# A fused linear-attention and mixture-of-experts layer: the state faded by two diagonal matrix products on PE, the gate split in two products, one normalisation chain for two uses

## The chip, the cores and the metric

The kernel runs on one core of a Trainium2 chip. The metric is the device time of one execution in microseconds (us). Engines are named as in the profile: PE (TensorE), PEld (its weight loads), DVE (VectorE), ACT (ScalarE), POOL (GpSimd) and SP (SyncE, which issues transfers).

## The reference, cut to what matters

The input x is 2 x 2048 x 256 in float32. A linear attention with a decaying state is followed by a gated mixture of experts (8 experts, two per token).

```python
def attn(out, W_write, W_read, decay, log_alpha):      # 4 heads of 64
    v = out @ W_write.T                                # values, per head
    # wk = out shifted by one token; M[p, q] = gamma**(p - 1 - q) where p > q
    # per chunk of tokens:
    #   reads = (W @ rk) * gamma**p  +  ((rk wk^T) * M) @ v
    #   W     = gamma**C * W  +  (v * gamma**(C-1-p))^T @ wk
    return out + (alpha * reads) @ W_read.T

def ffn(x, gate_w, w1, b1, w2, b2):
    probs = softmax(x @ gate_w.T)
    topk_probs, topk_idx = top_k(probs, 2)
    h = gelu(x @ w1[:, e] + b1[e])                     # for the two experts e
    return sum(topk_probs * (h @ w2[:, e] + b2[e]))

x = x + attn(layernorm(x))
x = x + ffn(layernorm(x))
```

## The kernel before, in words

The 2048 tokens of both batch rows are cut into 16 chunks of 128 tokens (`NCH = 16`); a chunk holds two matrices of 128 x 256. Stage one runs over the chunks as a software pipeline written out by hand. Each engine has a function `step(n)`, and in step n it works on several chunks at once: chunk n is normalised, chunk n-1 turned (transposed on PE), chunk n-2 goes through scores, values, state and reads, chunk n-3 through the read projection and the second layer norm, and chunk n-4 and n-5 through the gate, the choice of experts and the places of the rows in a sorted table in DRAM. Engines run their own queues in order and wait for each other by semaphores: `reached(engine, name, m)` waits until `name` has been signalled for chunk m.

Names that the text uses, with lines of the kernel before:

- `turn_chunk` (PE, L1546) transposes chunk n-1. `chunk_high` (ACT, L725) casts it to fp16, and `chunk_low` (DVE, L1036) computes what the cast left over; `last_column` is L736 and L738 on ACT. All products with three fp16 parts use such halves.
- `project` (PE, L1509) is the read projection, `residual` (DVE, L985) adds it, `residual_stats` (L992) and `residual_moments` (L1000) are the second layer norm's statistics.
- `values` (PE, L1573), `weigh` (PE, L1559) are values and scores; `weigh_scores` (DVE, L1052) multiplies scores with the decay table; `reads` (PE, L1592 and L1599) needs it and the state. `states` (PE, L1612) makes a chunk's contribution, `carry` (DVE, L1027) fades the state and adds it.
- `turn_normed` (PE, L1496), `normed_transposed` (ACT, L639), `score_experts` (PE, L1520) and `logits` (DVE, L1007) are the gate's product. `largest` (DVE, L891 to L897), `choose`, `exponential` (ACT, L654), `rank` (PE, L1533 to L1536), `place` (DVE, L960 to L978) follow.
- `normalise` (ACT, L673) and `chunk_normalise` (ACT, L702) apply the two layer norms; POOL makes their factors in a chain L546, L547, L549 (a power of -1/2), L551, once for each norm and step, and scatters rows to DRAM (L559).
- A weight split is the cast of 1024 columns of expert weights into two fp16 halves: `split_high` (ACT, L632) and `split_low` (DVE, L874). `PIECES` gives their number in each step: three in steps 3 to 7, two in steps 8 to 15, none in step 16.

PE's `step` issues, in this order, for the chunks named: turn_chunk(n-1), project(n-3), turn_normed(n-4), values(n-2), weigh(n-2), rank(n-5), states(n-2), score_experts(n-4), reads(n-2).

Stage two multiplies tiles of 256 or 128 sorted rows with the experts' weights (L1697 first layer, L1712 and L1714 second), in groups (`pair(f, z)`: group f of the first layer, group z of the second). Its first tiles use a table made after step 16 from the chunks placed by then. The last chunks' gate work stands between the first groups.

## Time and profile before

| what | value |
|---|---|
| median of three runs | 563.22 us (561.47 to 564.38) |
| profiled execution | 562.67 us |
| its span, first to last instruction | 560.9 us |
| PE busy | 530.1 us (95%) |
| DVE busy | 448.4 us (80%) |
| ACT busy | 338.3 us (60%) |
| POOL busy | 246.9 us (44%) |

The profiled execution's own time is 1.8 us over its span, the work around the program. Busy shares are means over two stages: up to about 167 us the chunks are worked on, and from there to the end PE multiplies with the experts' weights without a gap to speak of.

### The profile page before, as it was taken

The page shows a single profiled execution, that of the slowest core. Times are in us where ns is not written, and L with a number is a line of the kernel's source. Part 1 is how long each engine was busy: PE and PEld are TensorE (multiplying, and loading weights), DVE is VectorE, ACT ScalarE, POOL GpSimd, SP SyncE. Part 2 cuts the span into 40 slices and gives each one's busy share as a digit, 9 for nine tenths or more (in the row PEclk, how much of TensorE's full clock was granted, in tenths as well). Part 3 has the DMA queues.
Part 4 walks back from the last instruction along what each step waited for, and adds up shares of the span by engine and source line. Part 5 has one row for each costly group of instructions (what it writes and reads, how often), then busy time and mean ns, then how long its engine had stood idle before and what let it go on. Part 6 is the DMA issues. An engine that isn't in the chain of part 4 may idle for free.

```text
span 560.9 us, 17645 instructions
## 1 busy us (share of the span) xinstructions
PE 530.1 (95%) x5234; PEld 415.3 (74%) x5234; DVE 448.4 (80%) x1375; ACT 338.3 (60%) x856; POOL 246.9 (44%) x291
## 2 busy tenths in 40 slices
PE   7799899999999999999999999999999999999991
PEld 7677778778786777777777777777777777777770
DVE  4889999999987689868768787688777777778861
ACT  6899989898745876445545554455544544545540
POOL 5625778888746084523223233223322333322433
PEclk9999999999998999999999999999999999999997
DMA  5576867777345396433263364343344454344323
GB/s 161 201 229 225 258 185 234 210 222 231 126 105 129 87 216 101 71 60 62 51 103 56 53 105 77 63 68 61 61 63 79 78 78 75 68 64 67 63 37 36
DMA packets 85096, 63.33 MB, mean 113 GB/s; under 512 B 54224, under 2 KB 77392, under 8 KB 85008
## 3 DMA queue, kind: packets, MB, share of 16 engines
q1 hardware_dynamic: 71328, 43.94, 32.3%
q0 software_dynamic: 13392, 18.27, 17.3%
q8 instruction: 49, 0.80, 0.6%
q14 instruction: 39, 0.32, 0.2%
q10 hardware_dynamic: 288, 0.00, 0.0%
HBM read 37.56 MB, written 24.62 MB: 111 GB/s over the span
## 4 chain that ended last, share of the span: by engine, by line
PE 77%; DVE 10%; issue 4%; DMA 3%; ACT 2%; POOL 1%; SPq 1%; POOLq 0%; DVEq 0%; ACTq 0%
PE psum L1697 32%; PE psum L1712 21%; PE psum L1714 10%; PE psum L1509 3%; DVE weights L874 2%; PE psum L1592 2%; PE psum L1573 2%; PE psum L1599 2%; PE psum L1520 2%; DVE arena L1052 1%; PE psum L1559 1%; DMA arena<-sent_rows 1%; PE psum L1612 1%; PE psum L1496 1%; DVE arena L1063 1%
## 5 line engine op out<-in xcount | busy, mean ns | idle before, releaser
L1697 PE MATMUL psum<-arena,weights 128*128 128x256 f16 (+1 forms) x2208 | 279.7, 249 | 1.1 <-DVE arena L1316 1.0
L1697 PEld LDWEIGHTS psum<-arena,weights 128*128 x2208 | 187.4, 98 | 79.3 <-issue 4.1
L589 POOL DMA_INDIRECT out<-arena,tile_in x71 | 115.0, 1619 | 233.4 <-DVE arena L1343 126.9
L1712 PE MATMUL psum<-weights,arena 128*128 x556 | 211.7, 381 | 0.0
L826 ACT ACTIVATE arena<-psum,b_cur 128x256 f32<-128x256 f32 (+1 forms) x368 | 131.4, 423 | 129.9 <-PE psum L1697 115.6
L1714 PE MATMUL psum<-weights,arena 128*128 x556 | 152.0, 273 | 0.0
L1327 DVE TENSOR_TENSOR arena<-arena 128x512 f16<-128x512 f32 x142 | 98.5, 694 | 10.8 <-ACT arena L843 6.3
L559 POOL DMA_INDIRECT sent_rows<-arena,tiny x64 | 65.4, 1022 | 35.5 <-issue 17.8
L1323 DVE CAST arena<-arena 128x512 f16<-128x512 f32 x126 | 53.5, 424 | 8.8 <-ACT arena L826 8.5
L1712 PEld LDWEIGHTS psum<-weights,arena 128*128 128x128 f16 x556 | 54.4, 98 | 5.0
L1714 PEld LDWEIGHTS psum<-weights,arena 128*128 128x128 f16 x556 | 54.5, 98 | 4.6
L1309 DVE STREAM_TRANSPOSE tileT<-arena 128x512 f32<-128x512 f32 (+1 forms) x46 | 27.0, 586 | 37.1 <-DMA arena<-sent_rows 37.0
L647 ACT ACTIVATE arena<-tileT 128x512 f16<-128x512 f32 (+1 forms) x46 | 24.4, 531 | 49.8 <-DVE tileT L1309 49.8
L1339 DVE SCALAR_TENSOR_TENSOR arena<-psum,gate_scaled,arena 128x256 f32<-128x256 f32 x71 | 34.1, 480 | 15.5 <-PE psum L1714 13.8
L874 DVE SCALAR_TENSOR_TENSOR weights<-weights 128x1024 f16<-128x1024 f32 x32 | 38.5, 1215 | 2.0 <-ACT weights L632 2.0
L1509 PE MATMUL psum<-wrT,arena 128*128 128x256 f32 x128 | 31.7, 391 | 5.2 <-ACT arena L715 5.2
L1343 DVE SCALAR_TENSOR_TENSOR arena<-psum,gate_scaled,arena 128x256 f32<-128x256 f32 x71 | 34.4, 484 | 2.5
L632 ACT ACTIVATE weights<-weights 128x1024 f16<-128x1024 f32 x32 | 34.2, 1070 | 0.0
L836 ACT ACTIVATE arena<-arena,gate_cur 128x256 f32<-128x256 f32 x71 | 33.2, 506 | 0.0
L1509 PEld LDWEIGHTS psum<-wrT,arena 128*128 128x128 f32 x128 | 23.0, 190 | 10.9 <-ACT arena L715 8.3
L549 POOL TENSOR_TENSOR tiny<-tiny,minus_half 128x2 f32<-128x2 f32 x32 | 25.6, 800 | 2.7
L1316 DVE TENSOR_TENSOR arena<-tileT,arena 128x512 f16<-128x512 f32 (+1 forms) x46 | 25.8, 562 | 0.0
(199 smaller groups left out, 642.9 us busy)
## 6 DMA issues: line engine op xcount, KB each, us to landing
weights<-in_experts SPq DMA_DIRECT2D x32, 512.0 KB, 4.8
arena<-sent_rows SPq DMA_DIRECT2D x100, 64.0 KB
arena<-in_b SPq DMA_DIRECT2D x46, 128.0 KB, 3.2
arena<-in_x SPq DMA_DIRECT2D x16, 256.0 KB, 3.4
out<-arena SPq DMA_DIRECT2D x16, 256.0 KB, 4.1
arena<-sent_rows SPq DMA_DIRECT2D x84, 32.0 KB
sent_rows<-pad SPq DMA_DIRECT2D x7, 265.0 KB, 4.6
tile_in<-sent_rows SPq DMA_DIRECT2D x71, 4.5 KB, 2.6
```

Of the source, the lines that this page charges most:

```text
L559: pool.indirect_dma_start(out=sent, out_offset=bass.IndirectOffsetOnAxis(ap=at_bk, axis=0), in_=row[:, m % ROWS, b, :], in_offset=None).th ...
L589: pool.indirect_dma_start(out=out, out_offset=bass.IndirectOffsetOnAxis(ap=at_u, axis=0), in_=yout[:, u % 4], in_offset=None, compute_op=A ...
L632: a.activation(halves[:, j * 2 * PIECE:j * 2 * PIECE + PIECE], weights[:, (j + AHEAD) * PIECE:(j + AHEAD + 1) * PIECE], ACT.Copy, scale=WS ...
L826: last = a.activation(act[:, g % 2, m * n:(m + 1) * n], ps_h[:, g % 2, m * n:(m + 1) * n], ACT.Gelu_apprx_tanh, scale=1.0 / WSCALE, bias=b ...
L874: v.scalar_tensor_tensor(out=halves[:, j * 2 * PIECE + PIECE:(j + 1) * 2 * PIECE], in0=weights[:, (j + AHEAD) * PIECE:(j + AHEAD + 1) * PI ...
L1323: v.tensor_copy(h_hi[:, g % 4], act[:, g % 2]).then_inc(S2["hhi_done"], 1)
L1327: v.tensor_tensor(h_lo[:, g % 4], act[:, g % 2], h_hi[:, g % 4], ALU.subtract).then_inc(S2["split_done"], 1)
L1343: v.scalar_tensor_tensor(out=yout[:, u % 4], in0=ps_y[u % 4][:, 0], scalar=gate_scaled[:, u % 8:u % 8 + 1], in1=yout[:, u % 4], op0=ALU.mu ...
L1509: last = pe.matmul(ps_proj[:, b], readsT[:, s, b, k, 0:P], wrT[:, k], start=(k == 0), stop=(k == KD - 1))
L1697: last = pe.matmul(ps_h[:, f % 2, mm * n:(mm + 1) * n], w1_of(e_of[i], k, lo, per * (f - GROUP[i]) + mm), turned[:, i % 2, part, k, 0:n], ...
L1712: pe.matmul(to, h_hi[:, z % 4, at], w2_of(e_of[t], m), start=(m == 0), stop=(m == MF - 1), skip_group_check=True)
L1714: last = pe.matmul(to[:, 0], h_lo[:, z % 4, at], w2_of(e_of[t], m)[:, 0], start=False, stop=(m == MF - 1), skip_group_check=True)
```

## The change: what it does

1. The state. `carry` leaves DVE. PE multiplies the old state with a diagonal matrix of fading factors (`fade`, two products in float32) and accumulates in the same PSUM bank as `states`; ACT copies the sum to the state.
2. The gate. Its product is taken apart: the part of x goes through `gate_x`, twelve fp16 products with eight columns for a chunk (ahead of `turn_chunk` in PE's step), the part of the reads is eight more columns of the read projection (264 for 256). The rows need no mean, since it is taken out of the gate's weights at the start. ACT scales the first part (`scale_gate`), DVE adds the two (`logits`), and the exponential has the layer norm's factor as its scale, so it is two instructions for one. `turn_normed`, `normed_transposed` and `score_experts` go.
3. The gate's later work moves up by one step (`LAG` 4 for 5), since logits are there with the residual.
4. POOL makes the factors of both layer norms in one chain over four values, and two small values (`roots`, `sides`) behind it.
5. At the start: one more load (`wr_rows`), the gate's centring, halves and product with the read weights, and the fading tables.

```diff
-LAG = 5
+LAG = 4
...
             def step(n):
 
+                if active(n, 3):
+                    gate_x(n - 3)
                 if active(n, 1):
                     turn_chunk(n - 1)
                 if active(n, 3):
                     project(n - 3)
-                if active(n, 4):
-                    turn_normed(n - 4)
                 if active(n, 2):
                     values(n - 2)
                 if active(n, 2):
                     weigh(n - 2)
-                if active(n, 5):
-                    rank(n - 5)
+                if active(n, 4):
+                    rank(n - 4)
                 if 2 <= n <= NCH:
                     states(n - 2)
-                if active(n, 4):
-                    score_experts(n - 4)
                 if active(n, 2):
                     reads(n - 2)
...
+            def gate_x(m):
+
+                s = m % 2
+                reached(pe, "gate_x_done", m - 1)
+                reached(pe, "state_done", m - 1)
+                reached(pe, "xlo_done", m)
+                if m == 0:
+                    pe.wait_ge(gate_halves, 2)
+                for b in range(B):
+                    for at, (k, x, w) in enumerate(three):
+                        last = pe.matmul(ps_gate_x[:, b], xnT[:, x, s, b, k, 0:P], gate16[:, w, k],
+                                         start=(at == 0), stop=(at == len(three) - 1))
+                last.then_inc(S["gate_x_ps"], 1)
...
-                        last = pe.matmul(ps_state[d, b, h // 2], keys[:, s, b, cols], vals[:, b, cols],
-                                         start=True, stop=True)
+                        pe.matmul(ps_state[d, b, h // 2], keys[:, s, b, cols], vals[:, b, cols],
+                                  start=(b == 0 and h < 2), stop=True, skip_group_check=True)
+                for k in range(KD):
+                    last = pe.matmul(ps_state[:, :, k], fade[:, k], state[:, :, k], start=False, stop=True,
+                                     skip_group_check=True)
                 last.then_inc(S["state_ps"], 1)
...
+            def carry(m):
+
+                reached(a, "state_ps", m)
+                reached(a, "read_ps", m)
+                reached(a, "gate_x_ps", m)
+                a.activation(state.rearrange("p b k i -> p (b k i)"), ps_state.rearrange("p b k i -> p (b k i)"),
+                             ACT.Copy).then_inc(S["state_done"], 1)
+
+            def scale_gate(m):
+
+                reached(a, "gate_x_ps", m)
+                reached(a, "side_done", m)
+                reached(a, "logit_done", m - 1)
+                for b in range(B):
+                    last = a.activation(gate_x_part[:, b], ps_gate_x[:, b], ACT.Copy, scale=sides[:, m % 4, b:b + 1])
+                last.then_inc(S["gate_x_done"], 1)
...
                 if active(n, 1):
                     chunk_residual(n - 1)
-                if active(n, 5):
-                    exponential(n - 5)
+                if active(n, 3):
+                    carry(n - 3)
+                    scale_gate(n - 3)
+                if active(n, 4):
+                    exponential(n - 4)
...
-                reached(v, "logit_ps", m)
+                reached(v, "proj_ps", m)
+                reached(v, "gate_x_done", m)
                 reached(v, "top_at_done", m - 1)
-                v.tensor_copy(logit, ps_logit).then_inc(S["logit_done"], 1)
+                v.tensor_tensor(logit, ps_gate_read, gate_x_part[:], ALU.add).then_inc(S["logit_done"], 1)
...
                 if active(n, 3):
                     residual(n - 3)
+                    logits(n - 3)
+                if active(n, 3):
+                    residual_stats(n - 3)
+                    residual_moments(n - 3)
                 for j in splits(n)[0:1]:
                     split_low(j)
...
+            mean_gate()
             weigh(0)
             values(0)
             reads(0)
             states(0)
+            gate_through_reads()
             full_steps(step, 3)
```

DVE, in one step of the loop, from the residual to the score weighting. Before:

```order
L985 TENSOR_TENSOR arena<-psum,arena 128x512 [waits res_done,proj_ps]
L874 SCALAR_TENSOR_TENSOR weights<-weights 128x1024 [waits whi_done]
L992 BN_STATS tiny<-arena 128x6 [waits x1_done,moments2_done]
L992 BN_STATS tiny<-arena 128x6
L913 TENSOR_REDUCE tiny<-tiny 128x2 [waits exp_done]
L915 TENSOR_TENSOR tiny<-tiny,mask 128x16 [waits mask_done]
L1000 BN_AGGR tiny<-tiny 128x2 [waits ve2_done,stats2_done]
L1000 BN_AGGR tiny<-tiny 128x2
L1052 TENSOR_TENSOR arena<-psum,decayM 128x512 [waits read_ps,score_ps]
```

And with the change, at the same place of a step (L1061 is the logits' sum, L927 the weight split, L1096 the score weighting):

```order
L1038 TENSOR_TENSOR arena<-psum,arena 128x512 [waits res_done,proj_ps]
L1061 TENSOR_TENSOR tiny<-psum,gate_x_part 128x16 [waits top_at_done,gate_x_done,proj_ps]
L1045 BN_STATS tiny<-arena 128x6 [waits x1_done,moments2_done]
L1045 BN_STATS tiny<-arena 128x6
L1053 BN_AGGR tiny<-tiny 128x2 [waits taken,stats2_done]
L1053 BN_AGGR tiny<-tiny 128x2
L927 SCALAR_TENSOR_TENSOR weights<-weights 128x1024 [waits whi_done]
L966 TENSOR_REDUCE tiny<-tiny 128x2 [waits exp_done]
L968 TENSOR_TENSOR tiny<-tiny,mask 128x16 [waits mask_done]
L1096 TENSOR_TENSOR arena<-psum,decayM 128x512 [waits read_ps,score_ps]
```

The logits stand directly behind the residual now and wait for a signal of ACT, and statistics and aggregation stand ahead of the weight split.

PE, from the reads of one step to the values of the next. Before (L1546 turns the chunk):

```order
L1592 MATMUL psum<-arena 64x128 x8
L1599 MATMUL psum<-arena 64x128 x8
L1546 MATMUL psum<-consts,arena 128x128 x4
L1509 MATMUL psum<-wrT,arena 128x256 x4
L1496 MATMUL psum<-consts,arena 128x128 x4
L1573 MATMUL psum<-ww,arena 128x256 x12
```

With the change (L1668 and L1675 are the reads, L1578 the gate's product with x, L1622 the turning):

```order
L1668 MATMUL psum<-arena 64x128 [waits score_done,queries_done,read_done,state_done,val_done]
L1668 MATMUL psum<-arena 64x128 x7
L1675 MATMUL psum<-arena 64x128 x8
L1578 MATMUL psum<-gate,arena 128x8 [waits xlo_done,state_done,gate_x_done]
L1578 MATMUL psum<-gate,arena 128x8 x11
L1622 MATMUL psum<-consts,arena 128x128 [waits queries_done,xn_done]
L1622 MATMUL psum<-consts,arena 128x128 x3
L1595 MATMUL psum<-wrT,arena 128x264 [waits logit_done,base_done,x1_done,read_done]
```

Twelve products stand between the reads and the turning, and the four transposes behind the projection are gone.

## Rows read from the trace of the kernel before

**Rows 1.** Windows: us, busy and count of PE, PEld, DVE, ACT, POOL; clock, DMA, GB/s.

```profile
100.00:120.00 20.00, 18.98 (x240) 16.02 (x236) 19.36 (x79) 17.81 (x45) 16.02 (x26) 1.00 0.76 226
```

**Rows 2.** Timeline of DVE in one step: start, us, what, idle before with releaser.

```profile
93.17 0.69 DVE L1036 TENSOR_TENSOR arena<-psum,arena 128x512 f16<-128x512 f32 x1 [0.36 <-ACT arena L725]
...
94.50 0.68 DVE L985 TENSOR_TENSOR arena<-psum,arena 128x512 f32<-128x512 f32 x1
95.10 1.22 DVE L874 SCALAR_TENSOR_TENSOR weights<-weights 128x1024 f16<-128x1024 f32 x1
...
97.20 1.25 DVE L1052 TENSOR_TENSOR arena<-psum,decayM 128x512 f32<-128x512 f32 x2
...
99.09 1.21 DVE L874 SCALAR_TENSOR_TENSOR weights<-weights 128x1024 f16<-128x1024 f32 x1
...
101.51 0.59 DVE L1027 SCALAR_TENSOR_TENSOR arena<-arena,decayC,psum 128x128 f32<-128x128 f32 x2
...
102.91 0.69 DVE L1036 TENSOR_TENSOR arena<-psum,arena 128x512 f16<-128x512 f32 x1 [0.37 <-ACT arena L725]
```

**Rows 3.** Timeline of ACT in the same step and the next.

```profile
94.93 0.23 ACT L654 ACTIVATE tiny<-tiny 128x16 f32<-128x16 f32 x1
...
100.39 1.09 ACT L673 ACTIVATE arena<-arena,tiny 128x256 f32<-128x256 f32 x2 [1.09 <-POOL tiny L551]
...
111.55 0.61 ACT L725 ACTIVATE arena<-psum 128x512 f16<-128x512 f32 x1
```

**Rows 4.** Timeline of PE in these steps.

```profile
92.33 1.99 PE L1509 MATMUL psum<-wrT,arena 128*128 128x256 f32 x8 [0.66 <-ACT arena L715]
94.17 0.60 PE L1496 MATMUL psum<-consts,arena 128*128 128x128 f32 x4
94.60 1.48 PE L1573 MATMUL psum<-ww,arena 128*128 128x256 f16 x12
...
96.92 0.18 PE L1533 MATMUL psum<-mask,before 128*128 128x16 bf16 x1
...
97.01 0.17 PE L1536 MATMUL psum<-mask,ones 128*128 128x8 bf16 x1
...
107.46 1.06 PE L1520 MATMUL psum<-gateT,arena 128*128 128x8 f32 x8
108.46 1.09 PE L1592 MATMUL psum<-arena 128*64 128x128 f32 x16
...
110.50 0.66 PE L1546 MATMUL psum<-consts,arena 128*128 128x128 f32 x4
```

**Rows 5.** Timeline of POOL in the step.

```profile
95.72 0.68 POOL L546 TENSOR_SCALAR tiny<-tiny 128x2 f32<-128x2 f32 x1
...
96.76 0.72 POOL L549 TENSOR_TENSOR tiny<-tiny,minus_half 128x2 f32<-128x2 f32 x1
...
99.21 1.14 POOL L551 TENSOR_TENSOR tiny<-tiny 128x2 f32<-128x2 f32 x1
```

**Rows 6.** Timeline, a step in which PE's reads wait for the score weighting.

```profile
57.32 1.26 DVE L1052 TENSOR_TENSOR arena<-psum,decayM 128x512 f32<-128x512 f32 x2
...
58.84 1.09 PE L1592 MATMUL psum<-arena 128*64 128x128 f32 x16 [0.38 <-DVE arena L1052]
```

**Rows 7.** Timeline of PE, the reads in steps 3 and 15.

```profile
28.28 1.09 PE L1592 MATMUL psum<-arena 128*64 128x128 f32 x16 [0.31 <-DVE arena L1052]
...
147.20 1.09 PE L1592 MATMUL psum<-arena 128*64 128x128 f32 x16
```

**Rows 8.** Timeline of PE, turning chunk 2 at the start.

```profile
20.55 0.66 PE L1546 MATMUL psum<-consts,arena 128*128 128x128 f32 x4
```

**Rows 9.** Timeline of PE, the reads of step 16 and the first expert groups.

```profile
156.94 1.09 PE L1592 MATMUL psum<-arena 128*64 128x128 f32 x16
...
167.62 2.79 PE L1697 MATMUL psum<-arena,weights 128*128 128x256 f16 x24 [0.79 <-DVE arena L1316]
...
175.25 0.17 PE L1533 MATMUL psum<-mask,before 128*128 128x16 bf16 x1 [1.20 <-issue]
```

More of the change, by code:

```diff
@@ new lines, in step @@
+                if active(n, 0):
+                    reached(pool, "gate_x_done", n - 4)
+                    pool.tensor_tensor(roots[:], variances[:, 0:B], rs1[par], ALU.mult).then_inc(S["root_done"], 1)
+                    reached(pool, "root_done", n)
+                    pool.tensor_scalar(sides[:, n % 4], roots[:], 1.0 / WSCALE, 1.0 / WSCALE, ALU.mult,
+                                       ALU.add).then_inc(S["side_done"], 1)
+                if active(n, 4):
+                    m = n - 4
@@ L578, in add @@
                 if i == 0:
-                    pool.wait_ge(x1_out[0], 16 * 6)
-                    pool.wait_ge(x1_out[1], 16 * 5)
+                    for s in range(2):
+                        pool.wait_ge(x1_out[s], 16 * len(range(s, NCH - LAG, 2)))
                 if i == NE:
@@ L593, in _ @@
             step(NCH + 2)
+            add(0)
             step(NCH + 3)
-            add(0)
-            step(NCH + 4)
             for i in range(1, NT):
@@ L672, in normalise @@
                 for b in range(B):
-                    last = a.activation(row[:, m % ROWS, b, 0:D], res_of(m)[:, b], ACT.Identity, scale=rs2[:, b:b + 1],
-                                        bias=shift2[:, b:b + 1])
+                    last = a.activation(row[:, m % ROWS, b, 0:D], res_of(m)[:, b], ACT.Identity, scale=rs2_of(m)[:, b:b + 1],
+                                        bias=shift2_of(m)[:, b:b + 1])
                 last.then_inc(S["xm_done"], 1)
@@ L1019, in chunk_stats @@
                 last.then_inc(S["stats1_done"], 1)
-            def carry(m):
-                reached(v, "state_ps", m)
-                reached(v, "read_ps", m)
-                reached(v, "state_done", m - 1)
-                for k in range(KD):
-                    last = v.scalar_tensor_tensor(out=state[:, :, k], in0=state[:, :, k], scalar=decayC[:, k:k + 1],
-                                                  in1=ps_state[:, :, k], op0=ALU.mult, op1=ALU.add)
-                last.then_inc(S["state_done"], 1)
             def chunk_low(m):
```

276 lines of the change are left out of this document (155 added, 121 removed).

## The prediction, made before the kernel ran

> **What bounds the kernel now.** I read the busy time by windows first. Between 100 and 120 us three engines are nearly full: PE is busy 18.98, DVE 19.36 and ACT 17.81 of 20 us [rows 1]. So shares alone do not say what a removed instruction is worth, and I went to the timelines of one loop step. A step is the time from one low split of the turned chunk on DVE (L1036) to the next, 93.17 to 102.91: 9.74 us [rows 2]. Of it DVE idles 0.37 us, released by ACT L725, so its own work is 9.37 us. PE idles 0.66 us ahead of its projection [rows 4]. ACT idles 1.09 us ahead of L673 and is released by POOL L551 [rows 3], which took 1.14 us there [rows 5] while DVE L874 (99.09 to 100.30) ran.
>
> There is a circle through three engines. From L1036 (93.17) DVE comes to the score weighting L1052 at 97.20, 4.03 us later, and the two halves of it take 1.25 [rows 2]. The reads on PE can start 0.26 us after its end (57.32 + 1.26 to 58.84) [rows 6]. They last 2.04 (108.46 to 110.50), then comes the turning of the next chunk [rows 4]; from its start to ACT L725 are 1.05 us, L725 takes 0.61 [rows 3], and DVE follows about 0.03 later. Sum: 4.03 + 1.25 + 0.26 + 2.04 + 1.05 + 0.64 = 9.27 us, hardly less than the step. It is this circle that the change lengthens, and what DVE does after the weighting lies beside it.
>
> Over the loop the reads start at 28.28, and at 147.20 after 12 steps: 118.92 us, 9.91 each [rows 7]. Five of these steps split three pieces of the weights and seven split two.
>
> **The change part by part.** *DVE.* The fading of the state goes: L1027, two instructions of 0.59 us together, which overlap their successor a little, so I count 0.51 [rows 2]. It stands before L1036, outside the circle's DVE part, and so gives the circle nothing. The logits become one small sum instead of one small copy. But they move from the step's end to right behind the residual, into the circle: +0.09 us. The statistics now stand directly behind, and the aggregation waits for them with nothing in between; for that I add 0.12.
>
> *The wait of the logits.* They need `gate_x_done` of the same chunk, which ACT signals in the same step. ACT reaches the place of the new work where L654 stands, at 94.93 [rows 3], 1.76 us after L1036 at 93.17, since L725, a weight split and the residual come first. Then come the state's copy (half of L725, a copy of 128x512 from PSUM that takes 0.61: I take a slot of 0.28) and two small scalings (0.15 for the first's slot, 0.23 for the last, as L654 lasts). So the signal falls 1.76 + 0.28 + 0.15 + 0.23 = 2.42 us after L1036, and some 0.03 more to DVE. DVE wants the logits where L874 stands now, at 95.10, which is 1.93 [rows 2]. The wait is 0.52 us, in every step, with a bound of 0.3 (all three at the smallest slots) and 0.8 (none overlaps). Queued behind it on DVE are the statistics, a weight split and the score weighting, and PE's reads wait for that.
>
> *PE.* Transposing the normed rows (0.43 slot, 0.60 busy, L1496 at 94.17) and the float32 gate product (107.46 to 108.46, 1.00) go [rows 4]. Two fading products in float32 come, as many PE instructions as L1496 has, so 0.45. The state's copy loses nothing by them. Twelve fp16 products with eight columns come, ahead of turning the next chunk. The nearest rows are the rank products: L1533 at 96.92 and L1536, three later, at 97.01 [rows 4], 0.03 each; twelve give 0.36, and I take 0.40. The upper bound is L1573, whose twelve with 256 columns last 1.48 [rows 4]. PE's total falls, but PE waits 1.5 us for the weighting anyway; removed PE work is worth nothing in the loop, and the 0.40 stands in the circle.
>
> *The new circle.* DVE 4.03 + 0.09 + 0.12 + 0.52 = 4.76; 1.25; 0.26; 2.04; 0.40; 1.69. Sum 10.40 us. DVE's own work is 9.37 - 0.51 + 0.12 + the wait, 9.5 with two pieces and, with another L874 (1.13), 10.6; there the wait shrinks until both meet at 10.4. So all 12 steps take about 10.4: 124.8 against 118.92, **+5.9 us**.
>
> *POOL.* One chain instead of two serves both normalisations, with four values in a row where L549 had two (0.72 [rows 5]), and both now wait for the residual's moments. These end 3.6 us after L1036, just when DVE's weight split begins. L546 at 95.72 took 0.68 and ended 0.08 after the split that started at 95.10 [rows 2, 5], so I let the chain start when the split ends: L546 ends at 4.77, L549 starts 0.36 later and takes p, L551 follows at 5.21 + p. For p the ends are 0.72 (no growth) and 1.44 (double); L546 and L551, with the same shape but another operation, show that most of a small instruction is fixed, and I take 1.1. L551 ends at 6.5, ACT has waited about a microsecond, and its two normalisations (1.1 each, then 2.52 from L673 to L1036 as 100.39 to 102.91) end at 10.2: below the circle, so hidden.
>
> *Start.* Before the loop PE gets the fade (0.45), the gate through the read weights (four float32 products as L1520: 1.0) and 0.4 of gate products ahead of turning chunk 2, which starts at 20.55 [rows 8]. It would start at 22.40, and the reads of chunk 1, after 1.69 + 4.6 (4.76 without the gates' instructions of the first chunk) + 1.25 + 0.26, at 30.2 against 28.28: **+1.9**. The other new setup lies in idle time of DVE.
>
> *Step 16 and tail.* Step 16 has no splits, so neither wait nor circle binds, but PE: turning and gate products 3.1 after the reads, projection to rank 92.33 to 96.92 less the 0.43, weighting and signal 1.6. That is 8.9 for 9.74 (147.20 to 156.94): **-0.8** [rows 4, 7, 9]. From there to the first expert product (167.62) it is DVE's table and a load that decide, unchanged, 10.7. Behind it the gate product in front of the first mixed group, one turning and one more gate product leave PE's path while PE is full; the rank product at 175.25 waits for the residual, still 0.35 late at most: 0.43 + 0.9 + 0.35, **-1.7** [rows 9].
>
> Sum: +5.9 + 1.9 - 0.8 - 1.7 = +5.3 us. The profiled execution took 562.67, 0.5 less than the median 563.22; 568.0 from the one, 568.5 from the other. I forecast 568.3.
>
> **Rivals.** *The steps run at the engines' loads (faster).* If nothing of the circle binds, because the scalings come early and the gate products overlap the reads, DVE's work decides: 9.0 with two pieces, 10.1 with three. 7 x 9.0 + 5 x 10.1 = 113.5, -5.4; in all -6.0, 557 us. For it speaks that DVE is 97% busy now; against it the circle of 9.27, which DVE's saving does not touch. It decides only if the circle falls below 9.2. Chance 0.12.
>
> *The wait of the logits is hidden.* If ACT comes early enough, the circle is 9.88: 7 x 9.88 + 5 x 10.1 = 119.7, +0.8, in all +0.2: 563 us. For it: nothing but the modelled slots. Against it: ACT's queue, in which 2 us of work precede. Chance 0.15.
>
> *DVE's second weight split catches POOL's last instruction.* That split begins 1.81 after L1052 (97.20 to 99.09, less the logits' 0.08), at 6.57; L551 began at 99.21, after L874 at 99.09, and took 1.14 for its 0.20 [rows 2, 5]. With p over 1.36 this happens in each step. L551 then ends at 7.85 and the step takes 7.85 + 0.05 + 1.1 + 2.52 = 11.5, with three pieces 12.65: 143.8 in all, +24.8, 587 us. The Trainium skill, GPSIMD Engine Reference, section Key points, states that GpSimd shares its SBUF interfaces with VectorE and meets contention from instructions in a two-port mode or with two SBUF inputs. L874 has two, and the trace agrees with it by the 1.14. The rule speaks against a chain that is one and long. Chance 0.11.
>
> **How the numbers follow.** The forecast has 0.62, its own range 565 to 572 (a step of 10.1 to 10.7). The range is 561.5 to 576: below it lies the first rival, above it the third; 576 takes in gate products of 0.9 us. A measurement tells about 0.5%, 2.8 us. Faster: 0.13. Same: the second rival and the forecast's lower end, 0.18. Slower: 0.69.
>
> **What the profile would show.** DVE's logits idle 0.3 to 0.8 us, released by ACT's scaling; PE's reads idle over 1 us, released by the score weighting; 10.2 to 10.7 between low splits; POOL's L551 at 0.2 us; first expert product at 174 to 175. I am wrong if the logits do not wait, if the twelve products take over 0.8 us, or if ACT's chunk normalisation waits over 2 us for POOL.

## The result, and the profile after

| what | before | after |
|---|---|---|
| median | 562.35 us (559.97 to 564.38) | 577.4 us (575.76 to 579.49) |
| profiled execution | 562.67 us | 575.76 us |
| its span | 560.9 us | 574.0 us |
| mean granted clock of PE | 0.990 | 0.981 |
| PE busy | 530.1 us (95%) | 528.3 us (92%) |
| DVE busy | 448.4 us (80%) | 445.3 us (78%) |

The ratio is 1.027 (1.023 to 1.031), so the change costs 15 us. The forecast was 568.3, with 561.5 to 576.0 as its range. The direction was right, the size was not. In all tables a median is that of all executions, while a ratio leaves out those that took over 1.5% longer than the quickest of their kernel.

The windows of the kernel after, columns as in [rows 1]:

```profile
100.00:120.00 20.00, 16.63 (x214) 13.13 (x210) 15.67 (x64) 16.25 (x45) 13.39 (x18) 0.96 0.65 190
```

DVE was busy 19.36 of these 20 us before and is busy 15.67 now, so it idles 4.3 us. Where it waits is seen in the timeline of one step with two weight splits (start, us, what, idle before and its releaser). DVE:

```profile
113.55 0.69 DVE L1080 TENSOR_TENSOR arena<-psum,arena 128x512 f16<-128x512 f32 x1 [0.81 <-ACT arena L777]
...
116.11 0.17 DVE L1061 TENSOR_TENSOR tiny<-psum,gate_x_part 128x16 f32<-128x16 f32 x1 [0.55 <-issue]
...
118.44 1.28 DVE L1096 TENSOR_TENSOR arena<-psum,decayM 128x512 f32<-128x512 f32 x2
```

PE in the same step:

```profile
118.10 0.69 PE L1692 MATMUL psum<-arena 128*64 128x64 f32 x16 [1.13 <-ACT arena L744]
118.71 0.71 PE L1695 MATMUL psum<-arena,fade 128*128 128x128 f32 x4
119.98 1.09 PE L1668 MATMUL psum<-arena 128*64 128x128 f32 x16 [0.56 <-DVE arena L1096]
...
122.03 0.46 PE L1578 MATMUL psum<-gate,arena 128*128 128x8 f16 x12
122.34 0.63 PE L1622 MATMUL psum<-consts,arena 128*128 128x128 f32 x4
```

ACT in the same step (L682 are the gate's scalings, L753 is the next chunk's normalisation, L777 its cast after turning):

```profile
115.58 0.45 ACT L682 ACTIVATE gate_x_part<-psum,sides 128x8 f32<-128x8 f32 x2
...
120.20 1.09 ACT L753 ACTIVATE arena<-arena,tiny 128x256 f32<-128x256 f32 x2 [1.21 <-POOL tiny L579]
...
123.37 0.61 ACT L777 ACTIVATE arena<-psum 128x512 f16<-128x512 f32 x1
```

POOL in the same step, its chain for both norms:

```profile
117.49 0.96 POOL L573 TENSOR_SCALAR tiny<-tiny 128x4 f32<-128x4 f32 x1 [1.26 <-issue]
...
118.83 1.04 POOL L576 TENSOR_TENSOR tiny<-tiny,minus_half 128x4 f32<-128x4 f32 x1
119.95 0.21 POOL L579 TENSOR_TENSOR tiny<-tiny 128x4 f32<-128x4 f32 x1
```

The logits (L1061) idle 0.55 us. The view names no releaser, but ACT's second scaling (L682) ends at 116.03, and the logits start 0.08 us later; so it is in every step of the loop. The circle of the forecast can be added up from these rows: from the low split (L1080) to the weighting (L1096) 4.89; to the reads (L1668) 1.54; reads 2.05; gate products (L1578) 0.31; from the turning (L1622) to ACT L777 1.03; and 0.65 to the next low split. Sum 10.47 us, and 10.46 or 10.47 is the distance of the low splits in six of the eight steps with two pieces; of the others one ran in part at half clock (11.91, see below), and one took 10.81, with 0.28 us more of idle time on DVE that the trace puts down to nothing. The forecast had 10.40.

Two other things stand beside it. First, a step with three pieces takes 10.78 us, and there the reads do not wait for the weighting. ACT in one of them (L788 is the last column, L744 the values' copy):

```profile
68.92 0.42 ACT L788 ACTIVATE arena<-psum,decayQ 128x2 f32<-128x2 f32 x2 [0.21 <-PE psum L1622]
...
74.75 0.61 ACT L744 ACTIVATE arena<-psum 128x512 f32<-128x512 f32 x1
```

PE in that step:

```profile
75.41 0.69 PE L1692 MATMUL psum<-arena 128*64 128x64 f32 x16 [2.07 <-ACT arena L744]
76.03 0.71 PE L1695 MATMUL psum<-arena,fade 128*128 128x128 f32 x4
76.67 1.09 PE L1668 MATMUL psum<-arena 128*64 128x128 f32 x16
...
78.72 0.43 PE L1578 MATMUL psum<-gate,arena 128*128 128x8 f16 x11
```

This is a second circle, through ACT's queue. From the last column (L788, 68.92) to the copy of the values (L744, 74.75) are 5.83 us; 0.66 later the states (L1692); states and fade 1.26; reads 2.05; gate products and turning 0.98 to the next L788: 10.78. The fade stands in it with 0.64, the state's copy and the scalings in ACT's 5.83, the gate products with 0.31. DVE's own path is hardly shorter in such a step: DVE idles 0.55 us ahead of the logits and nowhere else, and is ready for its low split less than 0.1 us before ACT L777 lets it go.

Second, PE's clock. The reads of one step on PE:

```profile
53.49 1.90 PE L1668 MATMUL psum<-arena 128*64 128x128 f32 x16
55.33 1.90 PE L1675 MATMUL psum<-arena 64*64 64x128 f32 x16
```

Windows of ten microseconds, columns as in [rows 1] (the granted clock is the third number from the end):

```profile
28.00:38.00 10.00, 8.85 (x87) 7.28 (x88) 7.98 (x23) 7.91 (x19) 4.32 (x6) 0.83 0.72 217
50.00:60.00 10.00, 7.93 (x81) 6.39 (x82) 8.30 (x33) 7.82 (x19) 7.79 (x10) 0.83 0.53 152
60.00:70.00 10.00, 7.93 (x115) 6.60 (x115) 9.35 (x36) 9.44 (x27) 6.60 (x9) 1.00 0.74 245
```

The same windows of the kernel before:

```profile
28.00:38.00 10.00, 8.82 (x108) 7.45 (x108) 8.85 (x21) 9.90 (x24) 3.82 (x10) 1.00 0.70 215
50.00:60.00 10.00, 8.97 (x108) 7.26 (x106) 9.93 (x39) 9.43 (x23) 7.48 (x12) 1.00 0.79 259
```

Three times between 28 and 105 us the clock falls to 0.50 (1.2 GHz for 2.4), at about 30, 54 and 98, in steps in which PE had sat idle ahead of the states (1.88, 2.07 and 1.12 us). Reads that take 2.05 us then take 3.06 to 3.67, and these three steps lose 1.0, 1.6 and 1.4 us, by the distances of their reads. The other steps have the same idle time (2.07 or 1.12 us), and the clock does not fall in them. In the kernel before the windows from 28 to 170 us are at 1.00.

Reads and the first expert product after, to set beside [rows 7, 9]:

```profile
162.19 1.09 PE L1668 MATMUL psum<-arena 128*64 128x128 f32 x16 [0.55 <-DVE arena L1096]
171.04 1.09 PE L1668 MATMUL psum<-arena 128*64 128x128 f32 x16
...
181.48 0.72 PE L1780 MATMUL psum<-arena,weights 128*128 128x256 f16 x5 [0.91 <-DVE arena L1354]
```

The first reads of the loop start at 30.92. So the 13.1 us of span are: start +2.64, loop 131.27 for 118.92 (+12.35), step 16 8.85 for 9.74 (-0.89), then 10.44 for 10.68 (-0.24), and the rest 392.5 for 393.3 (-0.76).

### The profile page after: what moved, and what is told of

It reads as the page before. It is cut to its first block, busy times and chain, and to the rows that moved or that the text cites. A ratio compares the mean times of both kernels' runs of the same rounds, so it can differ in the third digit from the quotient of the medians.

```text
span 574.0 us, 17861 instructions
## 1 busy us (share of the span) xinstructions
PE 528.3 (92%) x5306; PEld 409.7 (71%) x5306; DVE 445.3 (78%) x1352; ACT 345.2 (60%) x904; POOL 252.0 (44%) x271
## 4 chain that ended last, share of the span: by engine, by line
PE 68%; ACT 8%; DVE 8%; issue 7%; DMA 3%; POOL 2%; SPq 1%; POOLq 0%; ACTq 0%; DVEq 0%
PE psum L1780 30%; PE psum L1795 19%; PE psum L1797 10%; PE psum L1668 3%; PE psum L1675 3%; ACT arena L801 2%; DVE arena L1096 2%; DMA arena<-sent_rows 2%; DVE weights L927 2%; ACT weights L665 1%; PE psum L1622 1%; ACT arena L735 1%; PE psum L1578 1%; DVE tiny L1045 1%; PE psum L1695 1%
## 5 line engine op out<-in xcount | busy, mean ns | idle before, releaser
L1365 DVE TENSOR_TENSOR arena<-arena 128x512 f16<-128x512 f32 x142 | 98.4, 693 | 11.9 <-ACT arena L896 7.4
L593 POOL DMA_INDIRECT sent_rows<-arena,tiny x64 | 67.5, 1055 | 35.1 <-issue 19.0
L927 DVE SCALAR_TENSOR_TENSOR weights<-weights 128x1024 f16<-128x1024 f32 x32 | 38.1, 1203 | 0.0
L1595 PE MATMUL psum<-wrT,arena 128*128 128x264 f32 x128 | 32.6, 397 | 0.0
L573 POOL TENSOR_SCALAR tiny<-tiny 128x4 f32<-128x4 f32 (+1 forms) x19 | 14.5, 761 | 38.5 <-DVE tiny L1053 18.6
L1692 PE MATMUL psum<-arena 128*64 128x64 f32 x240 | 10.3, 228 | 19.2 <-ACT arena L744 19.2
```

Of the source, the lines that this page charges most:

```text
L593: pool.indirect_dma_start(out=sent, out_offset=bass.IndirectOffsetOnAxis(ap=at_bk, axis=0), in_=row[:, m % ROWS, b, :], in_offset=None).th ...
L927: v.scalar_tensor_tensor(out=halves[:, j * 2 * PIECE + PIECE:(j + 1) * 2 * PIECE], in0=weights[:, (j + AHEAD) * PIECE:(j + AHEAD + 1) * PI ...
L1365: v.tensor_tensor(h_lo[:, g % 4], act[:, g % 2], h_hi[:, g % 4], ALU.subtract).then_inc(S2["split_done"], 1)
L1595: last = pe.matmul(ps_both[:, b], readsT[:, s, b, k, 0:P], wrT[:, k], start=(k == 0), stop=(k == KD - 1))
```

## The experiments

The experiments ran on five chips. On one of them, that of c1, the kernel before takes 563 us, as in the first measurement; the text calls it a chip of the first kind. On the four others it takes 574 to 578 us (the second kind). The kernels are therefore compared by their ratio to the kernel before, run beside them on the same chip.

| kernel | us | before beside it | ratio (95%) |
|---|---|---|---|
| c1, after | 578.5 | 562.7 | 1.028 (1.019 to 1.036) |
| e5, state's part alone | 566.6 | 562.7 | 1.008 (1.005 to 1.011) |
| e8, three moves | 567.6 | 562.7 | 1.007 (1.004 to 1.011) |
| g1, after | 614.7 | 576.6 | 1.064 (1.056 to 1.072) |
| e2, f2, g2, i2, logits late | 605.0, 609.8, 604.5, 603.3 | 576.6, 573.6, 576.6, 577.6 | 1.050, 1.052, 1.048, 1.040 |
| e3, f3, g3, PE filled | 603.4, 602.9, 606.9 | 576.6, 573.6, 576.6 | 1.047, 1.051, 1.052 |
| e4, state on DVE | 602.0 | 576.6 | 1.041 (1.033 to 1.048) |
| e1, f1, gate in the gap | 585.5, 580.9 | 576.6, 573.6 | 1.018, 1.012 |
| e10, i10, four moves and filling | 571.9, 574.8 | 573.6, 577.6 | 0.997 (0.995 to 0.999), 0.996 (0.993 to 0.999) |

Two more runs, h2 (the edit of e2) and h10 (the edit of e10), gave no result.

**e1 and f1: the gate products in PE's gap.** `gate_x(n - 3)` goes from the start of PE's step to its gap ahead of the states, as `gate_x(n - 2)`.

```diff
-                if active(n, 3):
-                    gate_x(n - 3)
...
                 if 2 <= n <= NCH:
+                    gate_x(n - 2)
                     states(n - 2)
```

> The changed kernel, but PE issues the twelve gate products of x one step earlier, in its idle time ahead of the state's products (1.12 us in a two-piece step), and no longer between the reads and the turning. Theory (the products stand in the circle reads, turning, high cast, low split, score weighting): from low split to low split 10.47 falls by the 0.32 that the products hold, until the chain over POOL and ACT binds at about 10.27; in three-piece steps 10.78 falls to about 10.45; in all 3 us less than the changed kernel, more where PE's shorter idle time keeps its clock. Rival (PE's work there is hidden behind ACT anyway): no change in the step.

> The twelve gate products moved from behind the reads into PE's gap ahead of the states, once more, because in the first run of this edit products behind the reads were slow on that chip. Theory (the products stand in both circles of the changed kernel): three-piece steps 10.78 to 10.4, two-piece steps 10.47 to 10.1, in all 4 to 5 us less than the changed kernel's 577 to 578.5. Rival (they are hidden): steps unchanged, within 1 us.

Steps with three pieces fell to 10.48 and 10.49 in the last three of each run, from 10.78. The first with two pieces took 10.0 in both (10.17 from reads to reads), and three later ones of f1 took 10.24 to 10.29, from 10.47; that is where e1's expectation had the chain over POOL and ACT bind, and in these three ACT does work without a gap from L753, which waits for POOL, to L788. The other two-piece steps took 10.35 to 13.4, at half clock or by the stall that g1 shows. So the products stand in both circles, with 0.3 us in the second and at least 0.2 in the first: the theory stands, its rival falls. Against the kernel before, the edited kernel is at 1.018 and 1.012, where the kernel after is at 1.064 on another chip of the second kind (g1).

**e2, f2, g2, i2: the logits behind the statistics.**

```diff
                     residual(n - 3)
-                    logits(n - 3)
                 if active(n, 3):
                     residual_stats(n - 3)
+                    logits(n - 3)
                     residual_moments(n - 3)
```

> The changed kernel, but DVE adds the logits behind the residual's statistics instead of ahead of them. Theory (the wait for ACT's scaled gate part, 0.55 us, and the bare wait between statistics and aggregation, 0.12, stand in the circle): DVE's logits no longer wait, two-piece steps go from 10.47 to about 9.8, three-piece steps stay near 10.78, since there another circle binds (ACT's casts up to the values, then the state's products and the fade on PE, then the reads); in all about 5.5 us less than the changed kernel. Rival (the steps are set by the chain over POOL and ACT, whatever the logits do): under 1 us less.

> The logits behind the residual's statistics, so that ScalarE's scaling has 0.75 us more before DVE wants it; once more on another chip than the first. Theory (the logits' wait binds the two-piece steps alone, the other circle through ScalarE's values and the fade the three-piece steps): two-piece steps 10.47 to 9.9 to 10.1, three-piece steps unchanged at 10.78, in all 3 to 4 us less. Rival A (the wait holds all steps): 0.5 us less in each, 6 us. Rival B (another wait takes its place): unchanged.

> The logits behind the residual's statistics. Theory (the logits' wait binds the two-piece steps): on a quick chip two-piece steps 9.9 to 10.1 for 10.47, three-piece steps unchanged, 3 to 4 us less than the changed kernel beside it. Rival (the edit itself brings PE's stall of 2 us behind the reads, by closing the gap ahead of them): steps of 12 to 14 us, 600 us and more on any chip, with the changed kernel at 577 to 580 beside it.

> The logits behind the residual's statistics. If the chip is a quick one (the kernel before at 560 to 565): theory (the logits' wait of 0.55 binds the two-piece steps) 9.9 to 10.1 us each and 572 to 576 us; rival (another wait takes its place) 10.4 to 10.5 each and 577 to 579. If it is a slow one (over 570): 12.3 us each and 600 to 610 again, and the question stays open.

Four runs, all on chips of the second kind. The logits no longer idle in any step of e2 and g2. Three three-piece steps (two of e2, one of g2) still took 10.78, as in the kernel after, and the first of g2 10.77 from reads to reads (10.40 between low splits): the logits' wait does not bind those. The two-piece steps took 12.0 to 12.4 at best, but for one of 11.24, and PE's stall (g1, below) covers what the wait was worth, so for them the question stays open. Beside the kernel after, on the same chip, the edit brought 614.7 down to 604.5; no run takes apart how much of that is the wait.

**e3, f3, g3: PE's gap filled.** Sixteen products of ones, whose result is not used.

```diff
                 if 2 <= n <= NCH:
+                    reached(pe, "state_done", n - 3)
+                    reached(pe, "gate_x_done", n - 3)
+                    for _ in range(16):
+                        pe.matmul(psum[:, 1, 288:288 + P], ones16[:], ones16[:], ...)
                     states(n - 2)
```

> The changed kernel with sixteen products of a constant added on PE in every step, ahead of the state's products, where PE idles for ACT; their result goes to unused columns. They take about 1 us of the 1.12 to 2.07 us of idle time. Theory (idle time in PE's queue lets its clock fall to half in some steps, at 1.4 us or so each, 4 us in the profiled execution): granted clock 1.00 up to the first expert product, no step over 10.9, about 4 us less than the changed kernel and less spread between its runs, although PE does more. Rival (the clock falls for another reason, or the slow steps have another cause): same time or up to 1 us more.

> The changed kernel with sixteen products of ones (0.9 us, their result is not used) in PE's gap ahead of the states; once more on another chip. Theory (the granted clock falls to a half because PE idles there, and this costs 1.0 to 1.6 us in each of three steps): no stretch at half clock between 28 and 170 us, all steps at 10.47 or 10.78, 3 to 4.5 us less than the changed kernel. Rival (the drops are random or come from elsewhere): they stay, and the filling costs nothing or up to 1 us.

> The changed kernel with sixteen products of ones in PE's gap ahead of the states. Theory (half clock comes from PE's idling there and costs 4 us): no stretch at half clock between 28 and 170 us, 3 to 4.5 us less than the changed kernel beside it. Rival (the edit itself brings PE's stall): steps of 12 to 15 us from the first two-piece step on, 600 us, on any chip.

In all three the three-piece steps took 10.78 to 10.82, each of them, with no stretch at half clock from 28 to 80 us, where the kernel after has 11.92, 10.79, 12.40, 10.77 and 10.78. A window of g3:

```profile
28.00:80.00 52.00, 46.57 (x629) 37.53 (x625) 48.49 (x174) 48.53 (x123) 36.26 (x45) 1.00 0.73 228
```

The same of the kernel after, and of g1, the kernel after on the chip of g3:

```profile
28.00:80.00 52.00, 42.57 (x534) 34.51 (x535) 45.84 (x160) 46.04 (x116) 35.00 (x43) 0.93 0.69 216
...
28.00:80.00 52.00, 40.87 (x514) 33.11 (x509) 44.74 (x157) 45.26 (x115) 33.10 (x42) 0.93 0.72 220
```

The same work at the same step's length, with PE 4 us busier: the clock then stays at 1.00, and the steps that lost 1.1 and 1.6 us (between low splits) lose nothing. All three traces of the unfilled kernel, the one after, c1 and g1, have two or three falls in that stretch; none of the three filled ones has any. For these steps the clock's loss is shown to come from PE's idling. The two-piece steps took 12.5 to 15 us in all three, again with the stall, and from 93 us on the clock falls there too, against the expectation; so for the fall at 98 us in the kernel after the cause is not shown. On the chip of g3 the filling brought 614.7 us down to 606.9.

**e4 and e5: the state's part undone, and alone.** e4 is the kernel after with the state faded by DVE as before. e5 is the kernel before with the two fading products on PE and the copy on ACT.

```diff
+                for k in range(KD):
+                    last = pe.matmul(ps_state[:, :, k], fade[:, k], state[:, :, k], start=False, ...)
...
                 if active(n, 3):
-                    carry(n - 3)
...
+            def carry(m):
+
+                reached(a, "state_ps", m)
+                reached(a, "read_ps", m)
+                a.activation(state.rearrange("p b k i -> p (b k i)"), ps_state.rearrange("p b k i -> p (b k i)"),
+                             ACT.Copy).then_inc(S["state_done"], 1)
```

> The changed kernel with the state faded and added by DVE as in the kernel before; the two fading products and ACT's copy are gone, the gate's part stays. Theory (DVE's fading lies ahead of the low split, outside the circle, while the copy delays ACT's gate signal by 0.27 and the fade delays the reads in three-piece steps by 0.6): two-piece steps 10.2, three-piece steps 10.5 to 10.6 (now DVE's own work), 3 to 4 us less than the changed kernel, clock aside. Rival (DVE's load sets the steps, so taking the fading off it was worth 0.5 a step): 6 us more than the changed kernel.

> The kernel before with the state's part of the change alone: two fading products on PE, the sum copied by ScalarE, DVE's two instructions gone. Theory (the state's part costs nothing by itself, because the reads wait for the score weighting behind it and the circle of low split, weighting, reads and turning does not hold it): steps of 9.7 to 9.9 us, ratio 0.995 to 1.005. Rival A (DVE's load bound the steps): 0.5 us less in each of 12 steps, ratio 0.99. Rival B (the fade and ScalarE's copy stand in the path): 0.6 to 1.1 us more in each step, ratio 1.013 to 1.023.

e5 ran on a chip of the first kind. It is 3.8 us slower than before by the medians, between the theory (nothing) and its rival B (7 us and more); its trace is of its quickest execution, 2.0 us longer than c2. Nearly all two-piece steps are 9.74 or 9.75, as before; three-piece steps 10.67 to 10.70 for 10.41 to 10.43, the first two of each apart. In the last three of c2 DVE never idles, so its own work holds them; in those of e5 it idles 0.67 to 0.69 us ahead of the logits. PE in one of these in e5 (states, fade, the gate's product, reads; L702 is ACT's copy of the values):

```profile
59.07 0.69 PE L1617 MATMUL psum<-arena 128*64 128x64 f32 x16 [0.92 <-ACT arena L702]
59.69 0.71 PE L1620 MATMUL psum<-arena,fade 128*128 128x128 f32 x4
60.23 0.96 PE L1522 MATMUL psum<-gateT,arena 128*128 128x8 f32 x8
61.12 1.09 PE L1594 MATMUL psum<-arena 128*64 128x128 f32 x16
```

And in the kernel before on that chip (c2):

```profile
56.59 0.69 PE L1612 MATMUL psum<-arena 128*64 128x64 f32 x16
57.20 1.06 PE L1520 MATMUL psum<-gateT,arena 128*128 128x8 f32 x8
58.64 1.09 PE L1592 MATMUL psum<-arena 128*64 128x128 f32 x16 [0.38 <-DVE arena L1052]
```

Before, the reads wait for the weighting and have 0.38 us to spare. With the fade the states wait for ACT's values, and from there the fade, the gate product and the reads follow without a gap. The second circle is born there. e4, on a chip of the second kind, came out at 1.041 where the kernel after has 1.064 on another such chip. Its three-piece steps took 10.66 at best, for 10.78, and DVE never idles in them (busy 10.53 of 10.66 us): without the second circle DVE's own work, with the fading back on it, holds them, nearly as the theory had it (10.5 to 10.6). Its two-piece steps took 11.9 to 15 us, and say nothing.

**c1, c2, g0, g1: the two kernels beside the edits.**

> A control: the changed kernel once more, on the chip and beside the edits. The four edits of the first set came out at 585 to 605 us on a chip on which the kernel before took 576.6, and in each of them PE's gate products, 0.38 us from the end of the reads to their signal in the first loop steps, took 2.0 to 2.6 us from some step on. Theory: that belongs to the chip or to the changed kernel on it, so this run shows it too: some steps of 12 to 14 us, 590 us or more if it falls on that chip. Rival: it comes from the edits; then this run has steps of 10.47 and 10.78 us, 131 us from reads(1) to reads(13), and a ratio of 1.02 to 1.03.

> A control for the trace alone: the kernel before on the chip of this set. Theory (the slow PE is the chip's): a stall of 2 us somewhere on PE in some of its steps too, so that it takes over 570 us on that chip; rival (only kernels with the gate products behind the reads have it): steps of 9.74 us as in the first profile, and the 13 us more on the first set's chip lie elsewhere.

> The changed kernel, unedited, beside the next two. On a chip where the kernel before takes 560 to 565: 577 to 579 us, steps of 10.47 and 10.78. On a chip where it takes over 570: if PE's stalls behind the reads are the chip's, steps of 12 to 14 us in this kernel too and over 595 us; if they come from the edits, the same steps as before and 580 us at most.

> The kernel before, for its trace on this chip. Theory: on a chip where it takes over 570 us, the projection or the products behind the reads are longer than 1.93 us in some steps, by 0.3 to 2 us; on a quick chip its steps are 9.74 and 10.4 as in the first profile. Rival: the steps are the same on both kinds and the difference lies in the expert part.

c1 and c2 are like the first measurement. g1 is not: the change costs 38 us there. ACT in a two-piece step of g1, at its wait for the turned chunk:

```profile
135.74 0.16 ACT L766 ACTIVATE arena<-psum 128x4 f32<-128x4 f32 x1
138.41 0.42 ACT L788 ACTIVATE arena<-psum,decayQ 128x2 f32<-128x2 f32 x2 [2.52 <-remote]
```

PE just before:

```profile
133.98 1.09 PE L1675 MATMUL psum<-arena 64*64 64x128 f32 x16
135.01 0.46 PE L1578 MATMUL psum<-gate,arena 128*128 128x8 f16 x12
135.32 0.63 PE L1622 MATMUL psum<-consts,arena 128*128 128x128 f32 x4
```

ACT reads what L1622 writes. By the modelled ends of the profile PE is through at 135.95; ACT is let go 2.5 us later. In the loop of c1 there is no such wait. The trace's semaphore events put the delay on the first thing behind the reads: from the end of the reads to the end of the twelve gate products are 0.37 to 0.40 us in every loop step of c1, and 1.1 to 3.3 in g1 from the reads of chunk 4 on, 2.5 or more in most; the granted clock in the records is 1.00 at most of them. The clock costs more there too: up to the reads of chunk 13 it stands at half for 38 us, for 17 in c1 and 10 in the kernel after. So PE stalls behind the reads on these chips, and the rival that the edits bring the stall falls: it comes with the chip, and comes in the kernel after too. It is smaller where other work follows the reads: in f1, which has the turning there, the projection behind it ends 0.3 to 1.2 us late. In g0, the kernel before on that chip, steps of 9.64 to 9.75 stand beside some of 10.5 and one of 12.94, 13.7 us more span in all; and ACT's wait for the turned chunk is there in two steps, 1.2 us together. So the stall is a small part of what the kernel before loses there: 2.8 of the 13.7 us lie ahead of the loop, 5.3 in it, 2.8 ahead of the first expert product and 2.9 behind, and the clock stands at half for 13.7 us up to the last reads of the loop, for none in c2. What stalls PE, and what else differs between the chips, no run shows.

**e8, e10, i10: the order of the step.** e8 has the moves of e1 and e2, and the score weighting ahead of the first weight split. e10 and i10 also put all of ACT's splits behind the copy of the values, and ten products of ones ahead of the states up to step 8.

```diff
                     residual_moments(n - 3)
-                for j in splits(n)[0:1]:
-                    split_low(j)
                 if active(n, 4):
                     weigh_gates(n - 4)
                 if active(n, 2):
                     weigh_scores(n - 2)
+                for j in splits(n)[0:1]:
+                    split_low(j)
...
                 if active(n, 2):
                     chunk_values(n - 2)
-                for j in splits(n)[2:] if len(splits(n)) > 2 else splits(n)[1:]:
+                for j in splits(n):
                     split_high(j)
```

> The changed kernel with three instructions moved: the logits between the residual's statistics and their aggregation, the score weighting ahead of the first weight split, and the twelve gate products in PE's gap ahead of the states. Theory (the circle of low split, weighting, reads, turning binds the two-piece steps; without the logits' wait, the split of 1.2 us and the gate products it is 10.40 - 0.52 - 1.1 - 0.4 = 8.4): the steps fall to what the loads give, 9.5 to 10 us, 7 to 10 us less in the loop than the changed kernel beside it. Rival (another circle, through ScalarE's casts, the values and the states with the fade, holds them): the steps stay at 10.4 us, at most 2 us less.

> The kernel of e8_order_on_dve with two more edits: ScalarE's high splits all behind the values' copy, and ten products of ones on PE ahead of the states in steps up to 8. Theory (in that kernel ScalarE's queue from the casts to the values, 5.2 us, then states, fade and reads bind the two-piece steps at 9.58, and half clock costs 6 us in the three-piece steps): two-piece steps 9.2 to 9.35, three-piece steps 10.3 to 10.5 without losses, 557 to 560 us, under the kernel before. Rival (DVE waits then for the high splits, or POOL meets its weight splits): steps stay at 9.6 and above, 562 us or more.

> The edit with all four moves and the filling of e10_order_and_filled. On a quick chip: two-piece steps 9.2 to 9.6, three-piece steps 10.3 to 10.5 without half clock, 558 to 562 us, a ratio of 0.99 to 1.00. On a slow one: 9.95 and 10.54 again, ratio 0.997.

e8 is 11 us faster than c1 beside it, with 9.56 to 9.68 for a two-piece step, within the theory's 9.5 to 10. What holds it there is seen in three timelines. POOL, whose chain now meets no weight split at its start:

```profile
144.03 0.24 POOL L573 TENSOR_SCALAR tiny<-tiny 128x4 f32<-128x4 f32 x1 [0.55 <-ACT tiny L699]
```

PE in the same step:

```profile
145.31 0.69 PE L1692 MATMUL psum<-arena 128*64 128x64 f32 x16 [0.74 <-ACT arena L744]
145.93 0.71 PE L1695 MATMUL psum<-arena,fade 128*128 128x128 f32 x4
146.57 1.09 PE L1668 MATMUL psum<-arena 128*64 128x128 f32 x16
```

The states wait for ACT's values and the reads follow the fade at once, as in the second circle. But ACT in the same step:

```profile
146.63 1.09 ACT L753 ACTIVATE arena<-arena,tiny 128x256 f32<-128x256 f32 x2 [0.43 <-POOL tiny L579]
...
149.31 0.42 ACT L788 ACTIVATE arena<-psum,decayQ 128x2 f32<-128x2 f32 x2
```

ACT waits for POOL's last instruction, and from there to L788 has no gap. In most two-piece steps of e8 the turned chunk is ready almost 0.1 us before ACT comes to L788. So the path over POOL and the second circle are of nearly one length, 9.6 us, and that over POOL is the longer one in most of these steps. e8 still loses some 6 us to half clock between 52 and 80 us (steps of 12.05, 13.45 and 11.97), and starts its loop 3 us late. i10 has no half clock between 28 and 180 us, and its three-piece steps take 10.32 to 10.54. Its two-piece steps took 9.6 to 10.1, not the 9.2 to 9.35 that e10's theory had, with a projection that in some ends 0.35 us late; what holds the others was not taken apart. e10 and i10 beat the kernel before, by 0.3 and 0.4%, with intervals that just leave out 1, on chips of the second kind; on one of the first kind they weren't run.

## Why the prediction was wrong

*What bounds the kernel.* By the trace after, right for the steps with two pieces: circle 10.40 forecast, 10.47 measured, each of its terms within 0.15 (DVE's part 4.76, measured 4.89; gate products 0.40, measured 0.31; the logits' wait 0.52, measured 0.55). That the products stand in it e1 and f1 show; that the logits' wait does was read from the rows, and the runs that moved it alone do not settle it.

*"So all 12 steps take about 10.4".* This step failed. The steps with three pieces are bound by the second circle, at 10.78. The forecast put the fade in PE's idle time ahead of the weighting ("the state's copy loses nothing", "removed PE work is worth nothing in the loop") and did not follow the path that ends in the states: ACT's queue up to L744, then states, fade and reads. It had PE wait 1.5 us for the weighting; measured are 0.56 in two-piece steps and nothing in three-piece steps, and the rest of the idle time, 1.12 and 2.07 us, lies ahead of the states, for ACT's values. In [rows 6] the reads had 0.38 us to spare, less than the fade's 0.64. Of the twelve distances from reads to reads four are of 10.78 and eight of 10.47, which makes 126.9 for the 124.8 forecast: +2.1 us, 1.5 of it by the second circle and 0.6 by the 0.07 that the first one was short. e5 shows the effect by itself, 0.27 us a step; f1 shows the gate products in it.

*A term that was missing: PE's clock.* The forecast counted PE's idle time as free. It is 1.1 to 2.1 us ahead of the states in each step, and three times the clock fell to half behind it: 4.1 us in the loop, 0.5 at the start (the fade took 1.22 there, not 0.71). This is the largest term of the miss. The filled kernels show it for the three-piece steps, so for 2.6 of the 4.1 us. With one step of 10.81 the loop is 4.4 over its two step lengths.

*Start.* +1.9 forecast, +2.64 measured, 0.5 of the difference by the clock. *Step 16.* 8.9 forecast, 8.85 measured. *Tail.* -1.7 forecast, -0.76 measured, and -0.24 before it, where nothing was forecast. No run took this apart.

*POOL's chain.* Right: L576 took 1.04 where 1.1 was assumed, L579 ends some 6.6 us after the low split (6.5 forecast), ACT waits 1.21 us for it and is in time all the same. The rival with the second split catching it did not come; L579 is over at 120.16, and that split starts at 120.28, only 0.1 us later. What the forecast called hidden was so by 0.2 us only: in the two-piece steps of the kernel after ACT has a gap of 0.1 us ahead of L788, where its instructions otherwise overlap by 0.1, and f1 and e8 run into this path. The rule that the prediction cited (the Trainium skill, GPSIMD Engine Reference, section Key points) agrees with the trace: L573 takes 0.96 us while DVE's split, with two inputs from SBUF, runs, and 0.24 in e8, where it doesn't.

*The rivals.* Those with 563 and 557 us fell, since the wait and the circle are there. Of 13.1 us of span the forecast had 5.3; 1.5 are the second circle, 0.6 the first one's size, 4.4 the loop's clock and one longer step, and 1.3 the start and the tail's smaller gain (+0.74 and +0.94, less 0.3 from step 16 and what follows it).

*The signs.* None of the three signs of being wrong came: the logits wait, the twelve products take 0.31 us, and ACT waits 1.21 us for POOL. Those of being right came in part: the reads idle 0.56 us, not over 1, three-piece steps are over 10.7, and the first expert product comes at 181.5, not 174 to 175. The signs watched the circle that was forecast, and none of them watched the path into the states or the clock.

*What stays open.* Whether the two-piece steps would fall to 9.9 to 10.1 by the logits' move alone; why the clock fell at 98 us; the start and the tail; and what PE's stall is. That stall is no part of the 15 us, but on the chips that have it the change costs 38.

## What to carry to other kernels

When an instruction is put into an engine's idle time, follow each path that ends behind it, not only the one that ends last now: the slack of the next one (0.38 us here) is the most that is free. PE's idle time is not free either: with gaps of 1 to 2 us in each step, three of twelve steps lost 1.0 to 1.6 us to the clock, more than the 0.55 us of the logits' wait. And a rearrangement that removes work can lose by its order; here three moved pieces of work gave back 11 us of 16 on one chip and, with a fourth and the filling, all of it on two others (0.3 and 0.4% under the kernel before).

## What the runs showed of the hardware

- PE's granted clock fell to half in three loop steps in which PE idled 1.1 to 2.1 us ahead of the states, and not in nine others with the same idle time; with 1.2 us of it filled (0.85 left of 2.07 in g3) the clock stayed at 1.00 from 28 to 80 us, in three runs of three.
- On four of the five chips PE stalled behind the reads, which end a run of fp32 products (states, fade, reads), mostly by 2.2 us or more and mostly with the granted clock recorded as 1.00 (g1). The rows of PE do not show it, since their ends are modelled; the wait of ACT for PE's result does (2.52 us). Between the two kinds of chips lie 11 to 15 us for the kernel before and 36 for the kernel after; how much of it is the stall was not measured.
- Twelve products with eight columns in fp16 take 0.31 us on PE, 0.026 each.
- A POOL instruction on 128x4 takes 0.24 us alone and 0.96 beside a DVE instruction with two inputs from SBUF; a power with four values in a row 1.04, where two values took 0.72 [rows 5].
